# Adjacency product and layer norm: TensorE products of a constant before the first tile, and new written-out orders for the first ten tiles

## The reference

```python
mask = adj > 0
head = mask / max(sqrt(sum(mask * mask, axis=-1)), 1e-12)
inc = adj + head
y = x + (inc @ x) / sum(inc, axis=-1)
out = (y - mean(y)) / sqrt(var(y) + 1e-5)        # along the row
```

## Time and profile before

| | us |
|---|---|
| median of 3 runs | 425.17 |
| the three runs | 425.17, 425.68, 419.24 |
| the profiled execution | 418.96 |
| its span | 417.2 |
| PE busy | 390.9 |
| DVE busy | 374.3 |
| ACT busy | 372.5 |
| POOL busy | 337.8 |

### The profile page before, as it was taken

The page is one execution under the profiler, slowest core; times in us unless marked ns, Lnnn a source line. Parts: engine busy times, 40 slices in busy tenths (PEclk is TensorE's granted clock), DMA queues, the critical chain, the costliest instruction groups (busy, mean ns, idle before and its releaser), DMA issues.

```text
span 417.2 us, 8912 instructions
## 1 busy us (share of the span) xinstructions
PE 390.9 (94%) x2190; PEld 345.6 (83%) x2190; DVE 374.3 (90%) x756; ACT 372.5 (89%) x512; POOL 337.8 (81%) x248
## 2 busy tenths in 40 slices
PE   0279999999999999999999999999999999999994
PEld 0268789888888888888888888888888888888884
DVE  0669889999999999999999999999999999999941
ACT  4867699999999999999999999999999999998420
POOL 2210389899999999999999999999999999999860
PEclk9999999999999999999999999999999999999998
DMA  8999996567676666666676666666676666661100
GB/s 232 257 238 253 264 252 199 172 198 219 187 226 207 216 199 196 202 202 193 213 213 193 208 196 195 199 204 195 209 218 191 207 196 196 198 199 42 38 26 14
DMA packets 36175, 79.90 MB, mean 192 GB/s; under 512 B 9536, under 2 KB 17728, under 8 KB 36160
## 3 DMA queue, kind: packets, MB, share of 16 engines
q1 hardware_dynamic: 35776, 78.68, 64.8%
q10 hardware_dynamic: 384, 1.05, 0.9%
HBM read 75.50 MB, written 4.19 MB: 191 GB/s over the span
## 4 chain that ended last, share of the span: by engine, by line
PE 82%; DVE 7%; issue 4%; ACT 3%; POOL 2%; ACTq 1%; POOLq 0%; DVEq 0%
PE edge L996 43%; PE edge L1005 22%; PE edge L951 15%; DVE inc L613 3%; DVE incT L629 2%; POOL inc_split L468 1%; DVE x_split L589 1%; ACT sign_out L234 1%; ACTq L153 1%; ACT scaled L245 1%; PE sums L946 1%; POOL norm L487 1%; PE sums L925 1%; ACT L276 0%; POOL rstd L452 0%
## 5 line engine op out<-in xcount | busy, mean ns | idle before, releaser
L468 POOL TENSOR_TENSOR inc_split<-incT,inc_split 128x896 fp32r<-128x896 f32 x120 | 252.9, 2132 | 5.3 <-DVE incT L629 5.1
L996 PE MATMUL edge<-x_split,inc_split 128*128 128x512 f32 (+1 forms) x870 | 210.2, 393 | 0.0
L996 PEld LDWEIGHTS edge<-x_split,inc_split 128*128 128x128 f32 x870 | 156.9, 188 | 29.5
L613 DVE SCALAR_TENSOR_TENSOR inc<-raw,scaled 128x1024 f32<-128x1024 f32 x128 | 153.5, 1200 | 2.8 <-ACT scaled L245 2.8
L629 DVE STREAM_TRANSPOSE incT<-inc 128x1024 f32<-128x1024 f32 x128 | 155.6, 1226 | 0.3
L245 ACT ACTIVATE scaled<-raw,norm 128x1024 f32<-128x1024 f32 x128 | 141.7, 1109 | 14.4 <-POOL norm L487 9.7
L234 ACT ACTIVATE sign_out<-raw 128x1024 int8<-128x1024 f32 x128 | 133.5, 1043 | 1.9 <-DMA raw<-in_adj_dram 1.9
L1005 PEld LDWEIGHTS edge<-x_split,inc_split 128*128 128x128 f32 x840 | 104.8, 191 | 2.3
L1005 PE MATMUL edge<-x_split,inc_split 128*128 128x256 f32 x840 | 106.0, 283 | 0.0
L256 ACT CAST inc_split<-incT 128x896 fp32r<-128x896 f32 x90 | 82.0, 935 | 5.9 <-DVE incT L629 5.8
L951 PE MATMUL edge<-x_native,incT 128*128 128x256 f32 x256 | 63.5, 389 | 2.5 <-DVE incT L629 2.4
(11 more groups left out here) (35 smaller groups left out, 135.7 us busy)
## 6 DMA issues: line engine op xcount, KB each, us to landing
raw<-in_adj_dram SPq DMA_DIRECT2D x504, 128.0 KB, 2.5
rows<-in_x_dram SPq DMA_DIRECT2D x32, 128.0 KB, 2.4
out_dram<-rows SPq DMA_DIRECT2D x32, 128.0 KB, 2.1
x_stage<-in_x_dram SPq DMA_DIRECT2D x8, 256.0 KB, 10.4
x_stage<-in_x_dram SPq DMA_DIRECT2D x8, 192.0 KB, 12.2
raw<-in_adj_dram ACTq DMA_DIRECT2D x8, 128.0 KB, 4.7
x_native<-in_x_dram SPq DMA_DIRECT2D x4, 128.0 KB, 6.4
```

Source lines behind the costliest of these rows:

```text
L468: nc.gpsimd.tensor_tensor(lo_of(s, q), incT[:, s, 0:SPLIT, q, :], hi_of(s, q).bitcast(fp32), ALU.subtract).then_inc(lo_by_pool, 1)
L613: nc.vector.scalar_tensor_tensor(inc[:, q, :], raw[:, s, q, :], 0.0, scaled[q % 2][:, :], ALU.is_gt, ALU.add, accum_out=part_sums[:, s, 0, ...
L996: last = nc.tensor.matmul(edge[s][:, c0:c1], inc_split[s][:, 0, b, :, :].rearrange("p q j -> p (q j)"), x_split[:, b, :, :].rearrange("p h ...
```

## The change

- Sixteen products of a constant (`warm_up`, 128x128 by 128x128, fp32, `quad_sum` with itself, into columns of `edge[0]` that nothing reads) stand on PE between the sums of tiles 0 and 1.
- PE multiplies tile 0's chunks 0 to 17, then tile 1's four native chunks, then tile 0's chunks 18 to 31, then the rest of tile 1. The sums stand at other places among the chunks, and the banks of the first eight sums are other ones.
- DVE transposes tile 0's quarters sooner after making them, makes and transposes all of tile 1 before it splits x, and does the four splits and degree work after it.
- ACT signs tile 0's second quarter before it scales the first, and so on through the early tiles; normalise of tiles 0, 1 and 2 comes later.
- SP issues the residual rows of tile 0 after tile 2's quarters, no longer before them.
- The written-out order goes to tile 9; the loop begins with tile 10 (`Fori(5, ...)` for `Fori(3, ...)`). The quarter norms stay in tiles 0 to 5. The loop's body and the end are unchanged. In tiles 4 to 9 the sum for `sum_quadrants` stands at lo 0, hi 23, 19, 20, 15, 14 (before: hi 25, 18, then 12 in all).

```diff
-            load_residual(0, 0, False)
             for k in range(G):
                 load_quarter(2, 0, k, True)
+            load_residual(0, 0, False)
             load_residual(1, 1, False)
...
+            def warm_up():
+                nc.tensor.matmul(edge[0][:, D:D + P], quad_sum[:, :], quad_sum[:, :], start=True, stop=True)
...
             sum_early(0, 2)
+            warm_up()
             sum_early(0, 3)
+            warm_up()
...
             sum_early(1, 0)
+            warm_up()
...
             sum_early(1, 1)
-            sum_early(1, 2)
-            unsplit_chunks(0, 0, 0, B, {9: lambda: sum_early(1, 3), 18: lambda: sum_degree(0, 0)})
+            warm_up()
...
+            unsplit_chunks(0, 0, 0, 18, {2: lambda: sum_early(1, 2), 4: lambda: sum_early(1, 3)})
+            unsplit_chunks(1, 1, 0, 4, {1: lambda: sum_degree(0, 0)})
+            unsplit_chunks(0, 0, 18, B)
+            unsplit_chunks(1, 1, 4, B, {5: lambda: sum_early(2, 0), 8: lambda: sum_early(2, 1),
+                                        14: lambda: sum_early(2, 2), 17: lambda: sum_early(2, 3),
+                                        25: lambda: sum_early(3, 0), 28: lambda: sum_early(3, 1),
+                                        31: lambda: sum_degree(1, 1)})
+            sum_early(3, 2)
+            tile(2, 0, {("hi", 6): lambda: sum_early(3, 3), ("hi", 15): lambda: sum_early(4, 0)}, first=True)
...
+            tile(4, 0, {("native", 0): lambda: [sum_early(5, 2), sum_degree(3, 1)], ("hi", 9): lambda: sum_early(5, 3),
+                        ("lo", 0): lambda: sum_quadrants(4, 0, early=True)})
+            tile(5, 1, {("hi", 23): lambda: sum_quadrants(5, 1, early=True)})
+            tile(6, 0, {("hi", 19): lambda: sum_quadrants(6, 0)})
...
-            with pe.Fori(3, PAIRS - 1) as u:
+            with pe.Fori(5, PAIRS - 1) as u:
```

More of the change, by code:

```diff
@@ L358, in _ @@
             scale_quarter(6, 0, 1)
-            with act.Fori(3, PAIRS - 2) as u:
+            sign_early(7, 1)
+            scale_quarter(6, 0, 2)
+            sign_early(7, 2)
+            sign_early(7, 3)
+            scale_quarter(6, 0, 3)
+            round_quarter(6, 0, 0)
+            sign_quarter(8, 0, 4, 0)
+            normalise(3, 1, 1)
+            round_quarter(6, 0, 2)
+            scale_quarter(7, 1, 0)
+            scale_quarter(7, 1, 1)
+            round_quarter(6, 0, 3)
+            sign_quarter(8, 0, 4, 1)
+            scale_quarter(7, 1, 2)
+            sign_quarter(8, 0, 4, 2)
+            sign_quarter(8, 0, 4, 3)
+            scale_quarter(7, 1, 3)
+            round_quarter(7, 1, 0)
+            round_quarter(7, 1, 2)
+            sign_quarter(9, 1, 4, 0)
+            normalise(4, 0, 2)
+            scale_quarter(8, 0, 0)
+            scale_quarter(8, 0, 1)
+            round_quarter(7, 1, 3)
+            sign_quarter(9, 1, 4, 1)
+            sign_quarter(9, 1, 4, 2)
+            scale_quarter(8, 0, 2)
+            sign_quarter(9, 1, 4, 3)
+            scale_quarter(8, 0, 3)
+            normalise(5, 1, 2)
+            sign_quarter(10, 0, 5, 0)
+            sign_quarter(10, 0, 5, 1)
+            round_quarter(8, 0, 0)
+            scale_quarter(9, 1, 0)
+            round_quarter(8, 0, 2)
+            round_quarter(8, 0, 3)
+            scale_quarter(9, 1, 1)
+            sign_quarter(10, 0, 5, 2)
+            scale_quarter(9, 1, 2)
+            sign_quarter(10, 0, 5, 3)
+            round_quarter(9, 1, 0)
+            scale_quarter(9, 1, 3)
+            sign_quarter(11, 1, 5, 0)
+            sign_quarter(11, 1, 5, 1)
+            scale_quarter(10, 0, 0)
+            normalise(6, 0, 3)
+            round_quarter(9, 1, 2)
+            round_quarter(9, 1, 3)
+            scale_quarter(10, 0, 1)
+            with act.Fori(5, PAIRS - 2) as u:
                 scale_quarter(2 * u, 0, 2)
@@ new lines, in _ @@
+            rstd_of(5, 1)
+            low_quarter(7, 1, 1)
+            low_quarter(7, 1, 2)
+            low_quarter(7, 1, 3)
+            norm_of(9, 1)
+            low_quarter(8, 0, 0)
+            rstd_of(6, 0)
+            round_quarter(8, 0, 1)
+            low_quarter(8, 0, 1)
+            low_quarter(8, 0, 2)
+            low_quarter(8, 0, 3)
+            norm_of(10, 0)
+            round_quarter(9, 1, 1)
+            low_quarter(9, 1, 0)
+            rstd_of(7, 1)
+            low_quarter(9, 1, 1)
@@ L540, in _ @@
+            low_quarter(9, 1, 2)
+            low_quarter(9, 1, 3)
+            with pool.Fori(5, PAIRS - 2) as u:
                 norm_of(2 * u + 1, 1)
@@ L793, in _ @@
-            transpose_quarter(5, 1, 3)
-            with dve.Fori(3, PAIRS - 2) as u:
+            transpose_quarter(6, 0, 0)
+            degree(4, 0)
+            inc_quarter(6, 0, 1)
+            inverse_degree(4, 0)
+            inc_quarter(6, 0, 2)
+            y_first(4, 0, 2)
+            shift_of(3, 1)
+            transpose_quarter(6, 0, 1)
+            y_second(4, 0)
+            count_of(7, 1)
+            statistics(4, 0)
+            transpose_quarter(6, 0, 2)
+            inc_quarter(6, 0, 3)
@@ new lines, in _ @@
+            transpose_quarter(7, 1, 3)
+            y_second(5, 1)
+            statistics(5, 1)
+            mean_variance(5, 1)
+            variance_eps(5, 1)
+            inc_quarter(8, 0, 0)
+            degree(6, 0)
+            shift_of(5, 1)
+            inverse_degree(6, 0)
+            inc_quarter(8, 0, 1)
+            y_first(6, 0, 3)
+            transpose_quarter(8, 0, 0)
+            inc_quarter(8, 0, 2)
+            y_second(6, 0)
+            transpose_quarter(8, 0, 1)
+            statistics(6, 0)
@@ L795, in _ @@
+            count_of(10, 0)
+            shift_of(6, 0)
+            statistics(7, 1)
+            transpose_quarter(9, 1, 2)
+            mean_variance(7, 1)
+            inc_quarter(9, 1, 3)
+            transpose_quarter(9, 1, 3)
+            variance_eps(7, 1)
+            with dve.Fori(5, PAIRS - 2) as u:
                 inc_quarter(2 * u, 0, 0)
```

259 lines of the change are left out of this document (152 added, 107 removed).

## The result

The changed kernel takes 422.27 us (median of 22 runs, 420.38 to 424.11), where 414.2 was forecast. Beside it, on the same chips, the kernel before gave 425.05 (22 runs). Its executions lie on two levels, 418.2 to 419.6 us and 424.6 to 425.7 us, and the comparison goes by the lower one: ratio 1.0084, interval 1.0065 to 1.0104. So against an execution of its own kind the change costs 0.8% and doesn't bring 1.1%. The profiled executions say the same: 422.05 us (span 420.3) against 418.96 (span 417.2). A second set of runs of both kernels (e9) gave the changed kernel 421.18 us and a ratio of 1.0026, with an interval that holds 1.

What follows compares the result with a forecast made beforehand. PE was taken as the bound, so the kernel gains what the start gains up to tile 7: 118.74 - 113.9 = 4.8 us, span 412.4, with 1.8 outside 414.2 us; range 412.5 to 415.2 (40%), wide 410.5 to 422.5.

Steps and rivals of the forecast that it cites:

- x decides the start: Tile 0 on PE: x piece 0 lands at 24.8 us, and PE waits about 1.4 us for it.
- PE is the bound: Tiles 8 to 29: PE's own work sets 11.71 us a tile, so an earlier start moves everything as a block.
- Tile 1's native chunks inside tile 0: Tile 1's four native chunks fill 30.8 to 32.8 us; without them PE would wait about 1.7 us for x piece 2.
- The chunk's 0.43 us: PE at full rate: four chunks take 1.73 us in a steady tile, 0.43 each.
- Tile 6's, with DVE's work unchanged between, comes 4.1 us and what DVE waited in between sooner: Tile 6's last transpose on DVE: earlier than 106.50 by that much; PE wants it 4.8 us sooner.
- The walk: Early tiles worked through in written order with assumed instruction times; tile 3's last transpose ends at 65.05 us, tile 4's at 78.0.
- x piece 0 landing after 26: Start of tile 0: a stated sign of being wrong, against the forecast landing at 24.8 us.
- A: Rival at tile 0: PE's clock is low at 24.8, so the 2.6 us are paid again; 416.5 us; 20%.
- B: Rival in tiles 2 to 5: norms come late behind POOL's low quarters, costing 1 to 3 us; 415.2 to 417.2; 25%.
- C: Rival, nothing gained: x lands later or DVE can't hold its 4 us; 418 to 420; 10%.
- D: Rival, slower: tiles 3 to 8 each miss a norm by 2.12 us; 12.7 lost, 4.8 gained, 427; 5%.
- The 4.8 us: The whole forecast gain: tile 7's start on PE moves from 118.74 to 113.9 us.

Runs made afterwards that it cites:

- e9: The changed kernel once more, unchanged, beside the kernel before and the one-read version on one chip: 421.18 us, ratio 1.0026.
- after: The changed kernel as first measured and profiled, against the kernel before: 422.27 us, ratio 1.0084.
- e1: Changed kernel with every shift made by tensor_scalar, reading one SBUF tensor and taking rstd as a per-partition scalar: 416.0 us, ratio to the kernel before 0.9912.
- e6: Changed kernel with the one-read shift, and tile 1's four native chunks put back behind tile 0's last chunk: 416.98 us, ratio 0.9934.
- e7: Changed kernel with the one-read shift, and tile 0's second and third quarter counts put ahead of making the quarters before them on DVE: 415.98 us, ratio 0.991.
- e8: Changed kernel with the one-read shift in tiles 0 to 6 only, two-read from tile 7 on: 416.06 us, ratio 0.9913.
- e11: Changed kernel with the one-read shift, plus the old two-read instruction into an unused spare tensor ahead of it in tiles 0 to 6: 422.48 us, ratio 1.0058.
- e2: Kernel before with the one-read shift in all tiles, nothing else changed: 418.9 us, ratio 0.9985.
- e12: Kernel before with the one-read shift only in tiles 0 to 2: 419.44 us, ratio 1.0002; its profiled execution took 424.06 us.

## Why the prediction was wrong

**The steps that held.** That x decides the start held: PE waits for x at chunk 4 in after, e1, e6, e7, e8 and e11 (0.51 to 2.04 us). That PE is the bound held behind tile 10, and once the shifts' waits are gone from tile 2 on (e1, e7). Tile 1's native chunks inside tile 0 start without a wait in after and e1, and cover a wait of 1.47 us (e6; worked out as 1.7). The chunk's 0.43 us and the sums of the tiles held too: with the shift repaired (e7), tile 7 starts 0.2 us from the forecast. Once DVE's waits are gone, the changed kernel takes 416.0 us, 1.8 above the forecast and inside its range; of this, 1.1 are there at tile 2 and still at tile 7 (x landed 0.7 later than the 24.8 worked out from the earlier trace rows), and 0.6 in the tiles behind 9 (12.08 and 11.92 us for tiles 9 and 10 in e1, in place of 11.71), which wasn't looked into.

**The step that failed** is the sentence "Tile 6's, with DVE's work unchanged between, comes 4.1 us and what DVE waited in between sooner". It shows first at tile 3, whose last transpose was worked out to end at 65.05: in after it ends at 67.70, behind the 1.98 us of the first shift, and in e1 at 65.66. DVE's instructions were unchanged, but their time wasn't: the shifts took 11.38 us in place of 5.50 up to 150 us. The walk priced `shift` as a small instruction beside the 1.2 us of the quarters. The page of before already had it at 739 ns for 128x1, beside 171 ns for the statistics' last step in nearly the same shape (128x2), and once at 1.36 us, until a low quarter of POOL ended. The question why a 128x1 instruction takes 739 ns wasn't asked. When instructions are moved against those of another engine, the part of their time that is waiting moves as well. Here, of the shifts of tiles 0 to 7, the new order has six that last 1.2 to 2.0 us and two of 0.8 and 0.9; the old one has one of 1.36, and the others last 0.15 to 0.81.

**Why the loss grew past the gain.** The prediction itself said that there is no reserve: ACT catches up at 0.37 us a tile, and DVE reaches tiles 4 and 6 "with tenths to spare". So of the 9.7 us that the shifts lose against e1 (11.38 - 1.65), 5.6 reach the end: the spans differ by 6.1, of which 0.45 was there at tile 2, ahead of the first shift. The 7.9 us by which the span misses the forecast (420.3 against 412.4) are then about 5.6 of shifts, 1.5 of x (tile 2 at 54.65, forecast 53.1) and 0.7 elsewhere, most of it behind tile 9. The prediction named "x piece 0 landing after 26" as a sign of being wrong, and it came: PE waits for it until 26.27 in after. It isn't what decided, since the other profiles of the changed order have it at 24.5 to 26.04, and e7 with 25.05 comes within 0.2 us at tile 7. The old order, 3.6 us later than e1 at tile 7, lost nothing by its 5.5 (e2). The gain of the start and the slack of DVE were the same microseconds: the change spent the slack, and what had been covered came out.

**The rivals.** A (the clock) fell: in after two chunks take 1.11 us from 24.19 on, inside the 24.8 that was said, and in e1 from 21.67 on. The rule of the Trainium skill that the prediction named for it, that a burst followed by a wait for DMA falls back, didn't bite here, with waits of up to 2.04 us in e7; the waits in that section's own example are longer than these, so it didn't speak against the forecast as strongly as the prediction took it. The one fall that a run shows came with 4.24 us of idle time (e12). B saw PE's idle time before natives, ended by DVE's transposes, in tiles 3 to 6, where 3 and 6 have it (and 8), but had its cause wrong: no norm came late behind a low quarter in a way that counted; it was DVE's own instruction. Its sign, ACT waiting for a norm, shows in tiles 0 and 1 alone (0.92 to 1.45 us) and not in tiles 2 to 6. C named the right engine ("DVE can't hold its 4 us", 418 to 420) and gave neither a mechanism nor the sign. D, the slower case, had a loss of 12.7 us at the norms; 5.6 were lost, at the shifts. The mechanism that decided wasn't among the rivals.

**Smaller terms.** The first chunk came at 22.33 and not at 21.2: a count stands behind the making of a quarter, so ACT waits 0.92 us for a norm twice (e7 takes one microsecond of it back), and the second sign waited 0.96 us for its data. A constant product took about 0.49 us at the lower level (2.91 us for six), priced at 0.45. The 4.8 us took tile 7's start of before from the chain (118.74); the timeline, from which tile 2's 57.29 comes, has it at 118.58, so the gain on one footing was 4.7. The unexplained second level of the kernel before was taken into the range as noise; it was a hint that some wait of 5 us hangs on chance, and e12 speaks for the same kind of wait as in the miss.

**What the chances were worth.** "Same" had 71% and came true by the bound of 2%, but with the opposite sign of the 1.1% forecast. The inner range, 412.5 to 415.2, missed. The wide one, 410.5 to 422.5, holds 422.27 by 0.2 us, and that is luck: it was made wide by A, B and the second level of before, and none of them made this time.

**Left open.** Why DVE gets the port after one low quarter in most executions and after three in others; why x's first piece lands between 24.5 and 26.3 us in executions of nearly the same program, which sets over 1 us of each; what the constant products are worth alone; and whether the upper level of the kernel before is what e12's one profile shows. The best of the kernels that ran is e1, 416.0 us, with e7 and e8 equal to it: 6.3 us below the changed kernel and 0.9% below the kernel before at its lower level.

## What to carry to other kernels

Look for instructions whose time doesn't fit their size, and ask what they wait for before moving anything: a wait inside an instruction doesn't show as idle time, and it changes with every new order. On DVE, give a per-partition column as the scalar of an instruction that reads one tensor in SBUF, not as its second tensor, wherever POOL is working beside it. And where a kernel's runs lie on two levels, look for a wait that depends on chance before forecasting a percent.

## What was new about the hardware

- A DVE instruction of 128x1 with two tensors in SBUF lasted 1.98 us until one instruction of POOL ended in after, and 5.53 us through three of POOL's in a row in e12, though POOL's second and third only started after it. In that execution it wasn't served in the order of arrival. The same product with one tensor and a scalar per partition took 0.21 us beside the same work of POOL.
- It holds in the other direction: in the kernel before, DVE's split of x (two tensors in SBUF) runs from 42.88 to 44.63, and POOL's two 128x1 norms beside it take 2.61 us together, where one takes 0.55 alone.

```profile
42.88 1.75 DVE L589 TENSOR_TENSOR x_split<-x_stage,x_split 128x1536 fp32r<-128x1536 f32 x1
```

```profile
43.05 2.61 POOL L487 TENSOR_TENSOR norm<-count,half 128x1 f32<-128x1 f32 x2 [11.79 <-DVE count L595]
```

- About 1.5 of the 3.53 us in which ACT waited for a norm in the earlier trace rows are this (2.61 less two times 0.55); the rest is the count, which stood behind an earlier split on DVE until 42.82. The prediction had rightly put the wait to the splits, without asking how a split on DVE makes a norm on POOL long.
- Idle time of 4.24 us on PE cost 1.5 us more behind it, by a granted clock of 0.60 over the next 3.6 us; behind the wait of 2.04 us in e7 the chunks ran on at 0.45 us each (28 records in 6.31).
